# A selective state scan beside a graph product: which four C products GpSimd makes (states 1, 3, 5, 8 instead of 1, 3, 8, 10)

## The reference, cut to what matters

```
h   = relu(adj @ layernorm(x) @ gcn_w + gcn_b);  h = layernorm(h) * ln_g + ln_b
xc, z = split(h @ w_in);  u = silu(causal_conv4(xc) + conv_b)
dt, B, C = split(u @ w_xp);  dt = softplus(dt @ w_dt + b_dt)
for every token t and state n (16):  hst[n] = exp(dt * A[n]) * hst[n] + dt * u * B[n]
y = sum over n of hst[n] * C[n];  y = (y + u * d_skip) * silu(z);  x = x + y @ w_out
x = x + lstm_block(layernorm(x))        # sequential, with a check pass
```

## Time and profile before

| | |
|---|---|
| median of the timed runs | 1586.23 us |
| profiled execution, own time | 1589.22 us |
| its span | 1587.4 us |
| granted TensorE clock, mean | 0.981 |
| busy: TensorE, VectorE, GpSimd, ScalarE | 95%, 86%, 71%, 65% |
| iterations 2 to 15 | about 130 to 1190 us |
| drain | about 1190 to 1320 us |

### The profile page before, as it was taken

The page is one execution under the profiler, slowest core; times in us unless marked ns, Lnnn a source line. Parts: engine busy times, 40 slices in busy tenths (PEclk is TensorE's granted clock), DMA queues, the critical chain, the costliest instruction groups (busy, mean ns, idle before and its releaser), DMA issues. The chain is left out here.

```text
span 1587.4 us, 17935 instructions
## 1 busy us (share of the span) xinstructions
PE 1510.1 (95%) x4975; PEld 771.2 (49%) x4975; DVE 1365.1 (86%) x1613; ACT 1027.2 (65%) x2183; POOL 1127.5 (71%) x541
## 2 busy tenths in 40 slices
PE   8999999999999999999999999999997788999995
PEld 3444434444444444444444444444442234999995
DVE  7405999999999999999999999999999896666998
ACT  3254757666676767676758576766666755776774
POOL 0325989898989898989889898989898862000223
PEclk9999999999999999999999999999997899999997
DMA  9877767777777777777777777777752422000002
GB/s 365 331 249 265 261 221 243 252 246 245 253 246 254 253 241 247 245 249 239 258 241 250 251 250 252 248 251 251 246 170 64 160 74 101 24 0 1 0 0 106
DMA packets 64956, 321.64 MB, mean 203 GB/s; under 512 B 6988, under 2 KB 7040, under 8 KB 31989
## 3 DMA queue, kind: packets, MB, share of 16 engines
q1 hardware_dynamic: 54001, 301.43, 54.9%
q10 hardware_dynamic: 10884, 19.41, 3.8%
HBM read 308.49 MB, written 12.32 MB: 202 GB/s over the span
## 5 line engine op out<-in xcount | busy, mean ns | idle before, releaser
L632 PE MATMUL bank<-ring,xh 128*128 128x512 f32 x2048 | 958.2, 595 | 12.5 <-DVE xh L1236 7.9
L1352 DVE TENSOR_TENSOR_SCAN work<-bank,hstate,work 128x512 f32<-128x512 f32 x512 | 627.6, 1267 | 21.5 <-ACT bank L927 16.6
L632 PEld LDWEIGHTS bank<-ring,xh 128*128 128x128 f32 x2048 | 388.6, 190 | 464.8 <-issue 424.3
L1115 POOL TENSOR_TENSOR work<-work 128x1024 f32<-128x1024 f32 x210 | 495.6, 2360 | 85.6 <-DVE work L1301 77.2
L927 ACT ACTIVATE bank<-work,a_neg 128x512 f32<-128x512 f32 x512 | 344.5, 686 | 249.8 <-DVE work L1352 245.9
L1293 DVE TENSOR_TENSOR work<-work,bank 128x1024 f32<-128x1024 f32 x256 | 309.6, 1214 | 63.0 <-POOL work L1091 54.4
L1301 DVE TENSOR_TENSOR work<-work,bank 128x1024 f32<-128x1024 f32 x168 | 200.8, 1195 | 21.1 <-POOL work L1115 21.1
L526 PE MATMUL bank<-bc_parts,sel 96*128 96x512 bf16 x425 | 163.8, 386 | 21.9 <-DVE work L1293 21.0
L1192 POOL TENSOR_TENSOR work<-work 128x256 f32 x32 | 27.3, 853 | 216.6 <-ACT work L988 216.6
L521 PE MATMUL bank<-work,w_sb 128*128 128x512 f32 (+2 forms) x352 | 175.8, 596 | 1.5 <-DVE work L1282 0.7
L1060 POOL TENSOR_TENSOR work<-work 128x1024 f32<-128x1024 f32 x48 | 113.7, 2368 | 19.4 <-ACT work L810 19.2
(11 more groups left out here) (151 smaller groups left out, 1580.5 us busy)
## 6 DMA issues: line engine op xcount, KB each, us to landing
ring<-adj_t SPq DMA_DIRECT2D x256, 1024.0 KB, 5.6
xh<-c_scratch SPq DMA_DIRECT2D x31, 256.0 KB, 3.3
work<-c_scratch ACTq DMA_DIRECT2D x28, 256.0 KB, 5.6
c_two<-c_scratch ACTq DMA_DIRECT2D x28, 256.0 KB, 5.8
xh<-x_rows SPq DMA_DIRECT2D x16, 256.0 KB, 6.4
work<-x_t SPq DMA_DIRECT2D x16, 256.0 KB, 5.3
x_scratch<-work ACTq DMA_DIRECT2D x16, 256.0 KB, 3.8
work<-x_scratch SPq DMA_DIRECT2D x1, 4096.0 KB, 13.1
```

Of the source, the lines that this page charges most:

```text
L632: last = nc.tensor.matmul(mixed[:, :], xn[:, j, :], a, start=(j == 0), stop=(j == BLK - 1))
L1115: nc.gpsimd.tensor_tensor(out=acc, in0=hc[0] if n == 1 else acc, in1=hc[n % 2], op=ALU.add).then_inc(y_added, 1)
L1352: nc.vector.tensor_tensor_scan(hb[s % 2][:, h, :], da[h], dbu[s % 2][:, h, :], hstate[:, HV * s + h:HV * s + h + 1], ALU.mult, ALU.add).th ...
```

## The change

GpSimd's product of state 10 becomes VectorE's, and VectorE's product of state 5 becomes GpSimd's. The loads of its rows are issued in slots 0, 2, 4 and 6 instead of 0, 2, 6 and 8, and so the third row is that of state 5 and the fourth that of state 8. `spread_c` passes over the states of `POOL_HC`, so that TensorE spreads row 10 and no longer row 5.

```diff
-POOL_HC = (1, 3, 8, 10)
+POOL_HC = (1, 3, 5, 8)
-C_LOAD = {0: 1, 2: 3, 6: 8, 8: 10}
+C_LOAD = {0: 1, 2: 3, 4: 5, 6: 8}
```

## The result

The changed kernel takes 1606.81 us (median of four runs, 1605.06 to 1609.24) against 1586.31: a ratio of 1.013, with a 95% interval of 1.0119 to 1.0142. The forecast was 1611. The profiled execution took 1606.02 us with a span of 1604.2.

The account below looks back on a forecast made before the run. Bound: a VectorE, ScalarE and GpSimd loop, not TensorE. Profiled 1589.2 + 21.6 (12 iterations at 1.8) + 3.0 (first two) = 1613.8 us; the median lies 3.0 lower, so 1611 us, range 1606 to 1616 (1597 to 1619 with rivals).

Parts of the forecast that it names:

- What bounds before: Iteration length is set by VectorE and ScalarE up to state 9 or 10, GpSimd's chain, product 15, next dBu; not TensorE.
- Product 10: On VectorE behind scan 11 it makes GpSimd's sum 10 even at best 0.4 us later; its VectorE slot costs about nothing.
- Product 5 and the silu: On GpSimd before tap 2: tap 3 and silu 2.33 us later, 0.46 slack, scan 9 1.87 late, sum 10 +1.8.
- The first two iterations: More slack before the silu there: a loss of 1.5 us each, 3.0 us together, instead of 1.8.
- The row loads: Load at slot 4 delays the ring's slot-6 piece by nothing or 1.2 us, hidden by TensorE's wait for u; counted as nothing.
- One sign of being wrong: Forecast wrong if the ring's slot-6 piece holds TensorE for over 1.2 us.
- The rule of the Trainium skill: A transfer over 127 partitions goes on a single engine, one over 128 is spread over sixteen; applied to the store at L423.
- What would show it: VectorE waits some 3 us before scan 9 (1.1 lead plus 1.87), TensorE about 1.1 for u; period 77.0 us.
- The faster one: GpSimd's end chain is relieved, silu and sum 10 do not move, TensorE then bounds: 1579 us; chance 0.08.
- The second, the smaller loss: Taps absorbed, but slot 4's load delays the slot-6 piece, or sum 10 is 0.4 us late: 1592 to 1599 us; chance 0.14.
- The clock's: New TensorE pauses bring its 1.2 GHz level each iteration: 6 to 13 us on top, 1617 to 1624 us; chance 0.06.
- Rival 4: Larger loss by TensorE's lower clock after new pauses: 1617 to 1624 us; chance 0.06.

Follow-up runs that it names:

- before, tap cut: Kernel before with the second tap sum cut to 8 of 512 columns of each half: 1586.3 us, ratio 1.0001.
- store split: Kernel before with only the store of 127 rows issued as two, of 112 and 15 rows: 1586.8 us, ratio 1.0006.
- small load: Changed kernel with the load of row 5 at slot 4 bringing 16 rows instead of 128: 1607.8 us, ratio 1.0132 against the kernel before.
- tap cut and small load together: Changed kernel with second tap sum of 8 columns and row 5 load of 16 rows: 1591.4 us, ratio 1.0036 against the kernel before.
- product 10 alone: Kernel before with product 10 given to VectorE, nothing taken in return, the load at slot 8 gone: 1593.5 us, ratio 1.0038.
- the two tap-cut runs: Changed kernel with second tap sum of 8 columns: with row 5 load also cut to 16 rows 1591.4 us, without that 1599.6 us.
- 5 for 8: Kernel before with products 1, 3, 5 and 10 on GpSimd, product 8 on VectorE, rows loaded at slots 0, 2, 4, 8: 1631.0 us, ratio 1.0286.

## Why the prediction was right

*What bounds before.* Right. Less work ahead of the silu changes nothing (before, tap cut), nor does a ring without delay (store split), while taking dtu out of the chain before sum 13 gives 0.8%.

*Product 10.* Right: "even at best it is 0.4 us later than now"; alone it costs 0.34 to 0.42 us of the period.

*Product 5 and the silu.* Right in place and nearly in size, and this path is the one that decides: with the ring's delay gone the time stays, with the silu on time it falls. But the ring is only 0.50 us an iteration behind it. The sizes: silu +2.30 (forecast 2.33), scan 9 +1.83 (1.87). Sum 10 then started 804.66 - 749.31 = 55.35 us into the iteration against 53.80 before (717.11 less a first dBu at 663.31): +1.55 and not +1.8. The term mis-sized is the way from scan 9 to product 10. From scan 9 to scan 10 went 3.83 us before (780.10 to 783.93) and 3.70 now (792.69 to 796.39), and from product 9 to scan 11 I took 2.40, where it is 2.26 (798.76 to 801.02): short waits were in what I took for VectorE's own pace, 0.27 us together. Twelve times 0.25 is 3 us of the 4 by which the forecast is high.

*The first two iterations.* +1.3 and +0.3 for 1.5 each. Iteration 3 took 76.44 us in the profile before, with the lower clock at its start, and 75.23 in that of the tap-cut control, where the granted clock from 211 to 216 us is 1.00. It is 1.00 in the changed kernel's profile too, and iteration 3 takes 76.76 us there. Against the control its loss is 1.5.

*The row loads.* "Either is hidden": right for the changed kernel (small load: no change). The delay itself is about 0.6 us, half of the upper bound, and it is not free: with the silu on time it costs 0.61 us. One sign of being wrong was met: the slot-6 piece held TensorE for over 1.2 us (1.21 to 1.26) in four of the twelve iterations. The small load shows that it was the wrong sign to name, since the time stays when that wait shrinks. The rule of the Trainium skill (DMA: Bandwidth & Descriptors, "Why a DMA increments its semaphore by 16 and not by 1") agrees with the runs: cut into 112 and 15 rows the store no longer holds the piece behind it, 7.6 us at most for 14.5. The bytes are the same, so bandwidth isn't what held it; which transfer engines carried the rows, no trace here shows.

*What would show it.* VectorE's wait before scan 9 is 1.57 us and not some 3. It came to scan 9 41.81 us into the iteration (43.38 - 1.57), 0.26 later than before, so its lead of 1.1 us was gone by then: 0.51 went to a B bank of TensorE, late from slot 6, and 0.60 before scan 7, which overwrites the buffer that product 5 reads on GpSimd. The forecast overlooked both; they cost nothing in the changed kernel, being ahead of a longer wait. But product 5 on GpSimd takes the lead away even with silu and ring on time. With tap cut and small load together (VectorE's timeline; L1354 is the scan there, L1139 the product) scan 7 waits 0.99 us for it, and scan 9 starts 41.71 us into the iteration against 41.55 before:

```profile
773.03 2.46 DVE L1354 TENSOR_TENSOR_SCAN work<-bank,hstate,work 128x512 f32<-128x512 f32 x2 [0.99 <-POOL work L1139]
```

TensorE waits 0.43 us for u and not 1.1, since the ring took the rest. Product 15's wait is 1.83, near what was worked out (1.38 + 1.8 - 1.3 = 1.88).

*The rivals.* None of their mechanisms decided. The faster one fails on product 10's place even without the taps (product 10 alone: 1593.5), and on scan 7's wait for product 5. The second, the smaller loss, names what is left once the silu is on time: its 1592 to 1599 us are the 1591.4 and 1599.6 of the two tap-cut runs. The clock's is answered in the last section.

## What to carry to other kernels

Before work goes to an engine with low average load, look at what stands behind the place in its queue: 2.33 us put in front of a sum that another engine waits for made that engine 2.30 us later, though GpSimd is idle 29% of the time. Several delays can hide one behind the other (here silu, ring and product 10), so taking one away shows its share only down to the next; take them away together and in turn. Where an engine waits once in each iteration for the end of a chain, move out of that chain what is needed later, before moving work to another engine.

## What the runs showed that I had not expected

A pause of TensorE of about 2 us at an iteration's start brought the lower clock in some iterations and not in others. With 5 for 8, at 371.29 and at 450.19 (TensorE's timeline):

```profile
371.29 0.39 PE L526 MATMUL bank<-bc_parts,sel 96*128 96x512 bf16 x1 [2.00 <-DVE work L1293]
371.52 3.19 PE L632 MATMUL bank<-ring,xh 128*128 128x512 f32 x4
...
450.19 0.39 PE L526 MATMUL bank<-bc_parts,sel 96*128 96x512 bf16 x1 [1.90 <-DVE work L1293]
450.42 1.88 PE L632 MATMUL bank<-ring,xh 128*128 128x512 f32 x4
```

The granted clock from 371 to 376 us is 0.66 (the 1.2 GHz level for part of it), from 449 to 454 it is 1.00 (columns as in the earlier trace rows):

```profile
371.00:376.00 5.00, 4.71 (x8) 2.08 (x9) 4.90 (x6) 1.74 (x4) 4.78 (x3) 0.66 0.19 28
449.00:454.00 5.00, 3.81 (x10) 1.82 (x11) 4.90 (x6) 2.26 (x5) 4.78 (x3) 1.00 0.30 68
```

Iterations with it took 78.9 us, those without 77.8: 1.1 us each. The pause's length does not tell them apart: one of 2.01 us at 763.61 us brought the lower clock (0.66 from 763 to 768), and one of 2.01 us at 998.14 did not (1.00 from 998 to 1003). What does, these runs don't show. Rival 4 is thus a real mechanism, seen here at pauses of 2 us and more; in the changed kernel's steady iterations no pause is longer than 1.3 us, and no slower spread or product follows one.
